# A decoder layer on one core: cross attention scores as one stacked contraction per pair of heads

## The reference, cut to what matters

```
x = x + recurrence(x)                         # stage A: linear recurrence over time
q = layernorm(x) @ wq.T + bq                  # stage B: cross attention, 16 heads of 16
k, v = ctx @ wk.T + bk, ctx @ wv.T + bv       # 77 keys
x = x + softmax(q*0.25 @ k.T) @ v @ wo.T + bo
h = layernorm(x); logits = h @ Wg.T + bg      # router, top 2 of 16 experts
x = x + sum over the 2 experts of rw * expert(h)   # stage C: gated MLP, 256 -> 512 -> 256
```

## Time and profile before

| | us |
|---|---|
| median of 3 runs | 776.34 (776.02 to 778.51) |
| the profiled execution | 782.94, its span 781.1 |
| PE busy | 619.5 (79%) |
| DVE busy | 486.6 (62%) |
| POOL busy | 337.2 (43%) |
| ACT busy | 321.9 (41%) |

### The profile page before, as it was taken

The page is one execution under the profiler, slowest core; times in us unless marked ns, Lnnn a source line. Parts: engine busy times, 40 slices in busy tenths (PEclk is TensorE's granted clock), DMA queues, the critical chain, the costliest instruction groups (busy, mean ns, idle before and its releaser), DMA issues.

```text
span 781.1 us, 13442 instructions
## 1 busy us (share of the span) xinstructions
PE 619.5 (79%) x3148; PEld 316.2 (40%) x3149; DVE 486.6 (62%) x1396; ACT 321.9 (41%) x723; POOL 337.2 (43%) x417
## 2 busy tenths in 40 slices
PE   1987887879999897979798963089999999999800
PEld 0666233523434242424252442045555555555400
DVE  4577226646487565856586645257777777777657
ACT  3854625226666464646465312023333333333300
POOL 4764714222644666467657236413333332333300
PEclk9999888569999898999899975579999999999955
DMA  9711000083000101010101001633333333333179
GB/s 321 260 11 12 0 1 0 5 296 108 1 3 17 41 14 43 11 47 0 55 7 49 21 34 55 177 54 93 84 89 78 90 85 85 87 90 86 40 281 364
DMA packets 93219, 62.37 MB, mean 80 GB/s; under 512 B 68186, under 2 KB 78558, under 8 KB 93056
## 3 DMA queue, kind: packets, MB, share of 16 engines
q1 hardware_dynamic: 85168, 44.04, 20.8%
q0 software_dynamic: 6864, 16.86, 6.3%
q10 hardware_dynamic: 1152, 1.06, 0.6%
HBM read 27.97 MB, written 25.56 MB: 69 GB/s over the span
## 4 chain that ended last, share of the span: by engine, by line
PE 43%; SPq 21%; DVE 12%; issue 10%; ACT 6%; DMA 3%; POOL 2%; another core or an unknown queue 1%; ACTq 0%; POOLq 0%; DVEq 0%
SPq L378 10%; PE bank L1023 5%; SPq L379 4%; SPq L374 4%; PE bank L852 4%; PE bank L981 3%; PE bank L877 3%; PE bank L1003 3%; PE bank L1005 3%; PE bank L841 3%; PE bank L1040 3%; PE bank L1054 2%; PE bank L1009 2%; PE bank L1007 2%; PE bank L895 2%
## 5 line engine op out<-in xcount | busy, mean ns | idle before, releaser
L583 POOL DMA_INDIRECT y_rows<-AR x79 | 76.9, 973 | 168.5 <-ACT AR L806 165.0
L486 POOL TENSOR_TENSOR W<-STG,W 128x512 f16<-128x512 f32 (+1 forms) x48 | 56.1, 1170 | 124.8 <-ACT W L611 123.6
L795 ACT ACTIVATE AR<-AR 128x256 f32<-128x256 f32 x79 | 32.9, 417 | 163.1 <-DVE AR L1570 151.5
L1396 DVE RECIPROCAL AR<-bank 128x512 f32<-128x512 f32 x16 | 53.7, 3353 | 41.8 <-PE bank L1023 33.5
L543 POOL DMA_INDIRECT xs_rows<-AR,SLOT x64 | 63.5, 993 | 27.3 <-issue 18.0
L711 ACT ACTIVATE AR<-bank 128x512 f32<-128x512 f32 (+1 forms) x80 | 47.6, 595 | 57.3 <-PE bank L1009 49.8
L1382 DVE TENSOR_REDUCE MX<-bank 128x4 f32<-128x308 f32 x128 | 56.7, 475 | 21.2 <-PE bank L981 14.4
L1570 DVE TENSOR_SCALAR AR<-bank 128x256 f32<-128x256 f32 x79 | 33.5, 425 | 54.6 <-PE bank L1149 52.1
L1146 PE MATMUL bank<-W,AR 128*128 x158 | 61.0, 386 | 0.0
L1147 PE MATMUL bank<-W,AR 128*128 x158 | 60.9, 385 | 0.0
L981 PE MATMUL bank<-KCUR,AR 128*128 (+1 forms) x128 | 42.5, 334 | 20.2 <-issue 8.8
(11 more groups left out here) (226 smaller groups left out, 1425.4 us busy)
## 6 DMA issues: line engine op xcount, KB each, us to landing
W<-in_wexp SPq DMA_DIRECT2D x16, 768.0 KB, 5.6
W<-y_rows SPq DMA_DIRECT2D x8, 1024.0 KB, 13.0
X<-in_x SPq DMA_DIRECT2D x4, 1024.0 KB, 12.2
out<-X SPq DMA_DIRECT2D x8, 512.0 KB, 8.6
CST<-in_cst SPq DMA_DIRECT2D x1, 1309.0 KB, 8.8
AR<-xs_rows SPq DMA_TRANSPOSE x79
AR<-xs_rows SPq DMA_DIRECT2D x79, 1.0 KB
y_rows<-AR POOLq DMA_INDIRECT x79, 2.4
```

The costliest lines, as they stand in the source:

```text
L486: pool.tensor_tensor(w[:, 1], STG[:, q], w[:, 0], ALU.subtract).then_inc(s["w_split"], 1)
L583: pool.indirect_dma_start(y_rows, bass.IndirectOffsetOnAxis(ap=NIX[:, k:k + 1], axis=0), CY[:, k, :], None, bounds_check=TOPK * NTOK - 1, ...
L1396: dve.reciprocal(AT[:, m], DEN[:, :]).then_inc(s["rec_s"], 1)
```

## The change

**Scores.** The three products and the minus-maximum term of two heads are laid on top of each other in the contraction. The new table KS holds, for each pair of heads and batch, 32 rows of high keys, 32 of low keys, 32 of high keys and 4 rows of ones and zeros; QS holds QH, QH, QL and the four rows of MT. One matmul over these 100 rows gives the finished scores of 64 keys of two heads (128 rows); the other 13 keys of four pairs make four matmuls of 32 columns into the four quarters of one bank (L1081). A half of the heads takes 4 + 4 matmuls instead of 20.

**By DMA.** QH, QL and MT can't be moved across partitions by an engine cheaply, so SP writes them to DRAM (`q_rows`, `m_rows`) and reads them back into QS: per group 4 writes and 6 reads for the queries, and 1 write and 2 reads for MT, each read after its write has landed. KS and the value tables VP, VR are laid out once for all batches by 35 DMAs in stage A. KCUR keeps its high part only, VCUR and IND go.

**Order.** PE's body now begins with router and output of the former groups, then four chunks of scores, `s1_turn`, the fifth chunk. A unit of maxima follows the first chunk of the second half, two follow each of the others, three lie within `s2_pv` and four behind it. On ACT `norm_q` goes ahead of the exponents, `evac_t` ahead of the weight pieces. The pieces are divided anew: 12 in stage A, 3 in each of 8 groups, 12 after stage B. PE's and SP's groups are written out instead of looped.

The diff, cut to its core:

```diff
-A_PIECES = 2 * PIECES
+A_EXP = 4
+A_PIECES = A_EXP * PIECES
+B_PIECES = A_PIECES + GROUPS * PIECES
+C_HALF = (B_PIECES + NPIECE) // 2
...
+            def q_stack(g):
+                first = g == 0
                 for m in range(DC):
+                    sp.wait_ge(s["ql_r"], 2 * g + (m + 1))
+                    if not first:
+                        sp.wait_ge(QSIN[m], g * QS_IN)
+                    for v, q in enumerate((QH, QL)):
+                        sp.dma_start(q_rows[m, v], q[:, m]).then_inc(QOUT[m], 16)
                 for m in range(DC):
+                    sp.wait_ge(QOUT[m], 32 * g + 32)
+                    if not first:
+                        sp.wait_ge(s["sc_mm"], g * (2 * NCH) - (1 - m) * NCH)
+                    for t, v in enumerate((0, 0, 1)):
+                        sp.dma_start(QS[32 * t:32 * t + 32, m], q_in[m, v]).then_inc(QSIN[m], 16)
+                sp.wait_ge(s["mT_r"], g + 1)
+                sp.dma_start(m_rows, MT[:, :]).then_inc(s["m_out"], 16)
+                sp.wait_ge(s["m_out"], 16 * g + 16)
+                for m in range(DC):
+                    sp.dma_start(QS[3 * 32:QROWS, m], m_in[m]).then_inc(QSIN[m], 16)
+
+            for g in range(GROUPS):
+                q_stack(g)
+                wload(g + (A_EXP + 2))
...
+            for n in range(A_PIECES // 2):
+                split(n, n % 2)
+            pool.wait_ge(s["a_kv"], 4)
+            pool.memset(CST[:, 0:B * DC * P], 0.0).then_inc(s["vr_z"], 1)
+            for n in range(A_PIECES // 2, A_PIECES):
                 split(n, n % 2)
             for u in range(4):
                 pool.wait_ge(s["vaq"], u // 2 + 1)
...
+            for n in range(B_PIECES, C_HALF):
+                split(n, n % 2)
             scatter(GROUPS - 1, 1)
+            for n in range(C_HALF, NPIECE):
+                split(n, n % 2)
...
+            def s2_scores(g, b, m, c):
+                if c == 0:
+                    pe.wait_ge(QSIN[m], QS_IN * (g + 1))
+                    if g == 0:
+                        pe.wait_ge(s["kv_in"], 16 * KV_DMAS)
+                if not (g == 0 and m == 0 and c < 2):
                     pe.wait_ge(s["exp_r"], g * (2 * NCH) + (m * NCH + c - 1))
-                pe.matmul(o, ind, MT[:, :], start=True, stop=False)
-                next(units, None)
-                pe.matmul(o, kh, QL[:, par, m], start=False, stop=False)
-                next(units, None)
-                pe.matmul(o, kl, QH[:, par, m], start=False, stop=False)
-                next(units, None)
-                pe.matmul(o, kh, QH[:, par, m], start=False, stop=True).then_inc(s["sc_mm"], 1)
-                next(units, None)
+                o = SC[(m * NCH + c) % 2]
+                if c < GT:
+                    mm = pe.matmul(o[:, :], KS[0:QROWS, m * GT + c, b, 0:P], QS[0:QROWS, m, c], start=True, stop=True)
+                else:
+                    for i in range(GT):
+                        mm = pe.matmul(o[32 * i:32 * i + 32, :], KS[0:QROWS, m * GT + i, b, P:PKW],
+                                       QS[0:QROWS, m, i], start=True, stop=True)
+                mm.then_inc(s["sc_mm"], 1)
```

More of the change, by code:

```diff
@@ L550, in body @@
                     add_bo(g)
-                if attn and nxt:
-                    for k in range(PIECES):
-                        split(g * (2 * PIECES) + (A_PIECES + k), k % 2)
+                if attn:
+                    for k in range(2):
+                        split(g * PIECES + (A_PIECES + k), (par + k) % 2)
                 if out:
@@ L557, in body @@
                     scatter(g - 2, par)
-                if attn and nxt:
-                    for k in range(PIECES, 2 * PIECES):
-                        split(g * (2 * PIECES) + (A_PIECES + k), k % 2)
+                if attn:
+                    split(g * PIECES + (A_PIECES + 2), par)
                 if out:
@@ L742, in body @@
                 first = isinstance(g, int) and g == 0
+                if nxt:
+                    for j in range(GT):
+                        norm_q(g + 1, j)
+                if log:
+                    pair_exp(g - 2)
                 if attn:
@@ L790, in _ @@
             pair_exp(GROUPS - 1)
+            for n in range(B_PIECES, C_HALF):
+                whi(n, n % 2, 16 * (n // PIECES + 1))
             def c_tanh(n, q):
@@ L1012, in s2_pv @@
             def s2_pv(g, b, m, units=iter(())):
                 pe.wait_ge(s["exp_r"], g * (2 * NCH) + (m + 1) * NCH)
-                if m == 0:
-                    pe.wait_ge(s["vcur_r"], b + 1)
-                if not (isinstance(g, int) and g == 0 and m == 0):
+                if not (g == 0 and m == 0):
                     pe.wait_ge(s["at_r"], 2 * g + m)
-                for o, w in ((NUM, VCUR[:, m]), (DEN, MV)):
-                    for v in range(2):
-                        for j in range(4):
-                            rows = P if j + v < NCH - 1 else LAST
-                            mm = pe.matmul(o[32 * j:32 * j + 32, :],
-                                           w[0:rows, j + v, v].rearrange("p a e -> p (a e)"),
-                                           PB[0:rows, j + v, :], start=(v == 0), stop=(v == 1))
-                        if (o, v) != (DEN, 1):
-                            next(units, None)
+                dmp, dmr = DMP[:, :, :].rearrange("p a e -> p (a e)"), DMR[:, :, :, :].rearrange("p i a e -> p i (a e)")
@@ new lines, in s2_pv @@
+                for o, whole, rest in ((NUM, VP[:, b, m * GT:(m + 1) * GT], VR[:, b, m]), (DEN, None, None)):
+                    for j in range(GT):
+                        w = dmp if whole is None else whole[:, j]
+                        mm = pe.matmul(o[32 * j:32 * j + 32, :], w, PB[:, j, :], start=True, stop=False)
+                    next(units, None)
+                    for j in range(GT):
+                        w = dmr[:, j] if rest is None else rest[:, 32 * j:32 * j + 32]
+                        mm = pe.matmul(o[32 * j:32 * j + 32, :], w, PB[:, NCH - 1, :], start=False, stop=True)
+                    if o is NUM:
+                        next(units, None)
@@ L1087, in body @@
                     for c in range(NCH):
-                        s2_scores(g, par, bp, 1, c, units if c >= 1 else iter(()))
+                        s2_scores(g, b, 1, c)
+                        for _ in range(2 if c else 1):
+                            next(units, None)
                     s2_pv(g, b, 1, units)
```

264 lines of the change are left out of this document (135 added, 129 removed).

## The result

The changed kernel takes 803.61 us (median of 4, 800.28 to 804.5), the kernel before, run beside it, 776.02 to 778.51 (a fourth execution, slow at 799.99, is left out of the comparison). The ratio is 1.035, 95% interval 1.032 to 1.038: slower by 3.5%, where 783 us were forecast and 797 was the upper end.

What follows compares the result with a forecast made beforehand. PE was taken as nearly full, with an ACT and POOL chain also bounding mid-group. Terms +2.5 + 6.0 - 3.9 + 1.0 + 1.0 = +6.6 on the median 776.3 gave 783 us; range 762 to 797, the forecast's own 779 to 788.

Steps and rivals of the forecast that it cites:

- The first half gains nothing: Steady group, first half of the heads: values begin at 14.3 us after the former group's values, against 13.9 before.
- The chain through ACT and POOL: Middle of a steady group: weight pieces behind s1_turn delay root, norm_3, queries' copy; first maximum at 27.8, loses 3.8 us.
- The clock at the second values: Second half of a steady group: clock falls in every group, 1.9 us taken, 3.7 if all values run at half.
- The clock at t = 0 to 5.4: After the former group's second values: thin PE work may halve the clock for router and output; 0.7 taken, up to 4.
- MT's DMA way, 0: Write and read-back of MT per group: 6.2 us hidden under 6.8 us of cover, cost 0, bounds 0 to 5.6.
- Rival 3: MT's DMA way is not covered: a 9 us round trip adds 18 us, 801 us; chance 0.05.
- Stage A and group 0, +2.5: Up to the end of group 0: later transposes and exposed DMA way against saved scores, sum +4.2, taken +2.5 us.
- Group 1, 37.5: Group 1 has a steady group's chain without router: 37.5 us against 31.5, +6.0.
- Tail, +1.0: From the last values to stage C: later weight pieces and scatter, mostly absorbed by the wait for rows, +1.0 us.
- rival 2: Clock falls twice and the unexplained gap lies on the path: group 41.0, kernel 798 us, middle 793; chance 0.13.
- the unexplained gap: PE waiting in steady groups that the profile before doesn't explain, 1.8 us each; 0 to 1.8 possible, 0.6 taken.
- The upper bound of 41.5 for a group: Steady group: forecast 38.5 us, bounds 35.3 if neither clock loss nor unexplained waiting falls, 41.5 if all of it.

Runs made afterwards that it cites:

- the eighteen matmuls: Changed kernel plus 18 useless PE matmuls behind the first score chunk of the second half, ahead of the first unit of maxima: 804.91 us.
- the run with sixteen matmuls: Changed kernel plus 16 useless PE matmuls per group between the end of the second values and the router: 782.51 us, ratio to before 1.009.
- the pieces moved: Changed kernel with stage A's first roots ahead of splits 6 to 11 and the tail's pieces, splits and last scatter reordered: 796.15 us.
- the second profile: The kernel before, unchanged, profiled once more: 776.6 us, groups 2 to 6 at 193.0 us.
- the run with both edits: Changed kernel with two weight pieces ahead of the exponents and 16 useless matmuls behind the second values: 760.52 us, ratio to before 0.982.

## Why the prediction was wrong

The sign was right, and so was the chain through ACT and POOL. What failed is the cost of the fallen clock at the router and output, and with it the time. Step by step:

- **The first half gains nothing.** Half right: values at 14.3 were forecast, they came at 18.6 (297.53 in group 3). Of the 4.3 us, 3.4 are router and output at half clock, 0.9 the transposes ahead of them (1.97 instead of 1.1).
- **The chain through ACT and POOL** loses 3.8 us: right. From the end of `evac_t` to the first maximum it was 12.0 us in the trace (298.46 to 310.49), 12.4 in the forecast (15.4 to 27.8), and taking the cause away gave 3.7. (By the forecast's own times PE would wait over 5 us there, not the 4 that it states; it waited 4.7.) The first maximum came at 31.6 and not 27.8 only because all of it stood 4 us later.
- **The clock at the second values:** sign right, 1.9 taken. Their first quarter took 1.52 instead of 1.06 in group 3, and recovering it bought nothing (the eighteen matmuls): less than 0.5. The total of this stretch came out near by luck: 3.6 + 1.9 = 5.5 were forecast and 5.2 measured (314.78 to 320.0), but even at full clock it is 5.3 in the run with eighteen, because three units of maxima, which the forecast put at nothing, stand between the quarters.
- **The clock at t = 0 to 5.4: the step that failed.** The forecast took 0.7, "a third of the 2 that I hold likely if it falls at all", and put "up to 4 more" into the bounds. Filling took it away: (204.7 - 188.1)/5 = 3.3 us per steady group and 5.6 in group 7, where 1.0 stood for half clock. 5 x (3.3 - 0.7) + (5.6 - 1.0) = 17.6 us of the time are this one term. A row for its size was there: of the two windows of the earlier trace rows with work that begins at half clock one is at 0.50, the other at 0.60, so router and output would pay most of their 5.6 us again (they paid 3.4), while the 2 came from no row. And it was averaged: the router took 3.59 us in four of the five steady groups and 3.09 in the fifth, the output 5.36 to 5.91, so a third was never a value that the cost could take. The Trainium skill, "TensorE: Matmul & The Clock Gate", section "HAM oscillation — how this bites in real kernels", tells of a matmul kernel in which each burst after a wait starts at half clock; the forecast named 41.5 us as the group by that rule, and the trace has 40.9. Without the term the forecast's group is 37.8, and the run with sixteen matmuls has 37.6; that they are so close rests in part on the luck of the second values.
- **MT's DMA way, 0:** right. In group 3 its write is issued at 283.15, its reads at 284.62, 1.47 us later instead of the 3.1 of a way; PE needs it at 293.68. The slower output gave it even more cover, but the run with sixteen matmuls, whose output is as fast as before, waits for it in group 0 only as well. Rival 3 falls.
- **Stage A and group 0, +2.5:** +1.0 measured. The first transposes came 3.3 us later than before (150.77 against 147.43), 3.1 forecast: right. The exposed DMA way cost 4.1 instead of 5.5. Scores and second half saved more than taken, though the clock was at half there too: with the pieces moved group 0 ends 8.4 us earlier, of which only 4.1 are the transposes.
- **Group 1, 37.5:** 38.2, right. **Tail, +1.0:** +2.2, of it some from DVE beside the splits. Of the signs named beforehand the clock (0.80), no wait for DMA into QS in the groups, group 1 and the tail (59) came as said; the first maximum (31.6) and the groups 2 to 6 (over 200) did not. The mean clock of 0.80 could not tell the forecast from rival 2, for which under 0.75 had been named.
- **Carrying the result over to the median.** I forecast whole groups from their parts (192.5), took the difference to one execution (196.4), and then lowered the sum by that execution's 6.6 us. But 3.4 of the 6.6 lay in those very groups, as the second profile shows. Against 193.0 the steady groups gain 0.5, not 3.9: the forecast should have been 786.
- **The chances.** Rival 2, in which the clock falls twice, was right in that and had 0.13. Its group of 41.0 against 40.9 is luck: it is the base of 35.3 with 1.9 at the second values, 2.0 at the router, where 3.3 was measured, and 1.8 of the unexplained gap, and PE's waits in the groups of the changed kernel show no such gap ahead of a unit. Its own time, 798, lacked group 7 and the error above. The upper bound of 41.5 for a group, called "all of it", is not that either: the forecast's own full costs, 3.7, 4 and 1.8 on 35.3, make 44.8.

Of the 23.7 us between the second profile of before (span 774.8) and the profile after (798.5), groups 2 to 6 have 11.7, group 1 6.6, group 7 5.9, group 0 and the tail 3.2, stage C -3.9 (each rounded). The last is not settled: stage C scatters by as much. The unexplained gaps of the earlier trace rows are not settled either; one of 2.0 us stands in the maxima stretch of the run with both edits, where DVE and ACT stood still as well.

## What to carry to other kernels

When matmuls are taken out of a schedule that PE nearly fills, ask for each thin stretch what dense PE work follows it and whether that work is on the path; cost it once at half clock and once at full, and carry both as cases, never a mean. At the router of the changed kernel every steady group paid (3.09 to 3.59 us instead of 1.85), but elsewhere it differs from pass to pass: the first half of the second values of the kernel before took from 1.93 to 3.15 us within one execution. An order that was balanced for the old amount of work has to be balanced anew: here moving two weight pieces gave 24 us and seven useless matmuls 21, and only both kinds of edit together (there with sixteen matmuls) made the change pay. A part that is forecast as a whole is compared with a typical execution, not with the one that happened to be profiled.

## What the runs showed of the hardware

- Useless matmuls can pay: seven per group ahead of the router, 1.67 to 3.03 us of PE, made the kernel 21 us faster; nine more ahead of them changed nothing that the medians show.
- PE's busy time rose when half of the score matmuls were left out (172.05 to 179.78 us in five groups, at a granted clock of 0.77 instead of 0.93).
- A small DVE operation beside POOL's elementwise work took up to 14 times its time: 2.73 us instead of 0.20 for 128x64, 1.16 instead of 0.17 for 128x16, and it ended with an operation of POOL's. The Trainium skill, "SBUF — State Buffer", section "Who interferes with whom", says that some DVE operations and GpSimd's lock one shared pair of ports for a whole instruction, while the other is blocked. The rows of the tail agree, down to the quick ones in POOL's pause. The 2.73 us go beyond one instruction of POOL's: they end with the last of four `add_bo` operations of 0.6 us each, and no run shows why DVE got no turn between them.
